# A new written-out order of the loop's tasks in an eight-element transformer layer

## The reference

```python
x = x + attn(layernorm(x))             # 16 heads of 16, two masked score entries, softmax over 512
x = x + xattn(layernorm(x), ctx_1024)  # own layernorm inside, 16 heads of 64, 64 keys, tanh(gate)
x = x + ffn(layernorm(x))
# ffn: a = entmax15(layernorm(x @ proj))             16 routing weights for each token
#      h = gelu(((xb @ Win1) * (a @ C1)) @ Wout1.T)  1024 wide, rank 128
#      y = ((hb @ Win2) * (a @ C2)) @ Wout2.T
```

## Time and profile before

| | |
|---|---|
| Time, median of 3 runs | 1042.75 us (1039.65 to 1044.42) |
| Profiled execution, its own time | 1039.97 us |
| Its span, first to last instruction | 1038.2 us |
| PE, DVE, ACT busy over the span | 94%, 74%, 59% |
| One turn of the loop | 114.2 us |
| Granted TensorE clock, mean over the span | 0.990 |

### The profile page before, as it was taken

The page is one execution under the profiler, slowest core; times in us unless marked ns, Lnnn a source line. Parts: engine busy times, 40 slices in busy tenths (PEclk is TensorE's granted clock), DMA queues, the critical chain, the costliest instruction groups (busy, mean ns, idle before and its releaser), DMA issues.

```text
span 1038.2 us, 15873 instructions
## 1 busy us (share of the span) xinstructions
PE 973.4 (94%) x5238; PEld 573.0 (55%) x5238; DVE 769.5 (74%) x1610; ACT 615.5 (59%) x857; POOL 150.7 (15%) x177
## 2 busy tenths in 40 slices
PE   5779999999989999999999999999999998999898
PEld 4434434556545645565556654565556554566676
DVE  3466756897799758985798759985898769737874
ACT  2336767555566666656665676656665675664533
POOL 2000000021012200221012100220021101311320
PEclk9889999999999999999999999999999999999999
DMA  6486885824420062112611061114411160023001
GB/s 168 119 254 218 256 262 175 266 50 122 91 75 22 11 170 56 52 32 46 179 51 30 11 182 51 31 31 124 100 51 31 30 174 21 1 82 82 1 1 42
DMA packets 77930, 97.38 MB, mean 94 GB/s; under 512 B 10383, under 2 KB 60370, under 8 KB 76850
## 3 DMA queue, kind: packets, MB, share of 16 engines
q1 hardware_dynamic: 77874, 96.69, 33.1%
HBM read 41.41 MB, written 29.36 MB: 68 GB/s over the span
## 4 chain that ended last, share of the span: by engine, by line
PE 62%; DVE 18%; ACT 7%; issue 6%; SPq 4%; DMA 2%; POOL 0%; ACTq 0%; DVEq 0%; POOLq 0%
PE y_ps L984 22%; PE x_ps L984 16%; PE pv_ps L984 7%; PE st_ps L984 7%; PE sm_ps L984 5%; DVE mx L1625 4%; PE y_ps L1147 3%; SPq L832 2%; ACT probs L1421 2%; PE y_ps L1113 2%; DVE stat L1645 1%; DVE qk_lo L1680 1%; DVE res L1697 1%; DMA a_scr<-a_cat 1%; ACT L1421 1%
## 5 line engine op out<-in xcount | busy, mean ns | idle before, releaser
L1625 DVE TENSOR_REDUCE mx<-sm_ps 128x2 f32<-128x1024 f32 x256 | 312.2, 1219 | 113.9 <-PE sm_ps L984 113.4
L1421 ACT ACTIVATE probs<-st_ps 128x1024 f32<-128x1024 f32 x256 | 262.4, 1025 | 178.0 <-PE st_ps L984 172.0
L984 PE MATMUL pv_ps<-probs,v_all 128*32 128x512 f32 x1024 | 135.9, 607 | 0.4 <-ACT o_t L1421 0.4
L984 PE MATMUL st_ps<-q_st,k_st 52*128 52x512 f32 x512 | 124.2, 480 | 2.1 <-ACT probs L1421 1.8
L984 PE MATMUL sm_ps<-k_st,q_st 50*128 50x512 f32 x512 | 118.5, 454 | 7.6 <-DVE mx L1625 5.3
L984 PE MATMUL x_ps<-b_cat,pt 128*128 128x256 f32 x448 | 112.0, 388 | 0.0
L984 PEld LDWEIGHTS st_ps<-q_st,k_st 52*128 52x128 f32 x512 | 48.4, 184 | 95.7 <-issue 55.0
L984 PEld LDWEIGHTS x_ps<-b_cat,pt 128*128 128x128 f32 x448 | 80.1, 190 | 23.9 <-issue 13.7
L699 POOL TENSOR_TENSOR px<-px,cst 128x512 f32<-128x512 f32 x56 | 58.1, 1044 | 202.2 <-DVE cst L1720 202.2
L984 PEld LDWEIGHTS sm_ps<-k_st,q_st 50*128 50x128 f32 x512 | 49.0, 186 | 69.5 <-DVE mx L1625 32.3
L1421 ACT ACT_TABLE_LOAD x60 | 77.0, 1283 | 1.8 <-PEq L2135 0.7
(11 more groups left out here) (304 smaller groups left out, 1708.3 us busy)
## 6 DMA issues: line engine op xcount, KB each, us to landing
a_scr<-a_cat SPq DMA_DIRECT2D x16, 1024.0 KB, 5.7
a_cat<-a_scr SPq DMA_DIRECT2D x8, 2048.0 KB, 8.6
q_st<-qk_hi SPq DMA_DIRECT2D x128, 64.0 KB, 2.3
k_st<-qk_hi SPq DMA_DIRECT2D x128, 64.0 KB, 2.2
b_scr<-b_cat SPq DMA_DIRECT2D x8, 1024.0 KB, 5.0
b_cat<-b_scr SPq DMA_DIRECT2D x16, 512.0 KB, 10.7
xa<-in_x SPq DMA_DIRECT2D x9, 512.0 KB, 3.9
q_st<-qk_lo SPq DMA_DIRECT2D x64, 64.0 KB, 2.2
```

The lines of the kernel that those rows point to most:

```text
L984: return nc.tensor.matmul(dst, lhs, rhs, start=start, stop=stop, **kw)
L1421: return nc.scalar.activation(dst, src, f, **kw)
L1625: nc.vector.tensor_reduce(mx[:, c % 2, 0:16].rearrange("p (m x) -> p m x", m=2)[:, :, col], sm_ps[:], axis=AX, op=ALU.max).then_inc(sm_tak ...
```

## The change

It puts the 179 entries of LOOP_PE, 83 of LOOP_ACT, 113 of LOOP_DVE and 13 of LOOP_SP in other orders; no entry is added or taken away. Two edits outside the lists: ScalarE, before it writes xt_hi in ON 0, waits for PJ 0 and Z1 1 of the element before (their matmuls read xt_hi); and the gated result of the very last step lies in px instead of in probs. EARLY_*, LAST_* and TAIL_* stay. In the new orders:

- TensorE: the OT, Y and ON steps move forward, QK0 moves from after M2 to after M7 and QK3 from before OT 2 to just ahead of M13. H0 moves from right behind P24 to behind QK 2 part 0. ZM5 to ZM7 now end the turn. 27 P and M pairs stand side by side instead of 26, and 10 P or M stand alone instead of 12.
- ScalarE: the Exp and Gelu users alternate less: 6 changes of table in a turn instead of 10.
- VectorE: EN1 and Z2 come ahead of M0, EN0 comes after M29.
- Queue: ST comes first; FS0 and FS1 after MR0; RS and FS2 now behind MR2; LA and LB now behind FS3, and MR3 behind these.

```diff
 LOOP_PE = (
-    ("P", 0, 0), ("M", 0, 0), ("V", 0, 0), ("V", 0, 1), ("V", 1, 0), ("V", 1, 1), ("X1", 0, 0), ("TN", 0, 0),
-    ("PV", 15, 0), ("P", 2, 0), ("M", 1, 0), ("X1", 1, 0), ("OT", 0, 0), ("P", 4, 0), ("M", 2, 0), ("QK", 0, 0),
...
-    ("M", 11, 0), ("G", 0, 0), ("P", 22, 0), ("G", 1, 0), ("PV", 4, 0), ("M", 12, 0), ("P", 24, 0), ("H", 0, 0),
-    ("P", 26, 0), ("M", 13, 0), ("PV", 5, 0), ("X2", 0, 0), ("X2", 1, 0), ("M", 14, 0), ("H", 1, 0), ("M", 15, 0),
...
+    ("M", 0, 0), ("P", 0, 0), ("V", 0, 0), ("V", 0, 1), ("TN", 0, 0), ("V", 1, 0), ("V", 1, 1), ("M", 1, 0),
+    ("X1", 0, 0), ("PV", 15, 0), ("M", 2, 0), ("P", 2, 0), ("OT", 0, 0), ("OT", 1, 0), ("X1", 1, 0), ("M", 3, 0),
+    ("P", 4, 0), ("OT", 2, 0), ("OT", 3, 0), ("P", 6, 0), ("M", 4, 0), ("PV", 0, 0), ("P", 8, 0), ("Y", 0, 0),
+    ("Y", 1, 0), ("P", 10, 0), ("PV", 1, 0), ("M", 5, 0), ("P", 12, 0), ("ON", 0, 0), ("ON", 1, 0), ("P", 14, 0),
+    ("M", 6, 0), ("PV", 2, 0), ("PV", 3, 0), ("P", 16, 0), ("M", 7, 0), ("QK", 0, 0), ("QK", 0, 1), ("P", 18, 0),
...
+    ("QK", 2, 0), ("H", 0, 0), ("H", 1, 0), ("QK", 2, 1), ("H", 2, 0), ("M", 12, 0), ("S", 0, 0), ("S", 0, 1),
+    ("S", 1, 0), ("S", 1, 1), ("P", 30, 0), ("S", 2, 0), ("S", 2, 1), ("S", 3, 0), ("S", 3, 1), ("QK", 3, 0),
+    ("QK", 3, 1), ("M", 13, 0), ("P", 32, 0), ("T", 0, 0), ("S", 4, 0), ("S", 4, 1), ("T", 1, 0), ("O", 0, 0),
+    ("M", 14, 0), ("P", 34, 0), ("PV", 7, 0), ("M", 15, 0), ("P", 36, 0), ("O", 0, 1), ("O", 0, 2), ("S", 5, 0),
+    ("S", 5, 1), ("O", 0, 3), ("P", 38, 0), ("M", 16, 0), ("T", 2, 0), ("S", 6, 0), ("S", 6, 1), ("TN", 2, 0),
...
+    ("PV", 13, 0), ("PV", 14, 0), ("M", 30, 0), ("P", 60, 0), ("Z1", 0, 0), ("Z1", 1, 0), ("P", 62, 0), ("M", 31, 0),
+    ("ZM", 5, 0), ("ZM", 6, 0), ("ZM", 7, 0))
...
 LOOP_DVE = (
...
+    ("EN", 1), ("Z2", 0), ("M", 0), ("TN", 0), ("EN", 2), ("EN", 3), ("M", 1), ("X1", 0), ("M", 2), ("OT", 0),
...
+    ("X2", 1), ("M", 11), ("QK", 2), ("M", 12), ("C", 0), ("C", 1), ("SU", 0), ("C", 2), ("C", 3), ("SU", 1),
+    ("QK", 3), ("SU", 2), ("M", 13), ("M", 14), ("C", 4), ("M", 15), ("C", 5), ("M", 16), ("SU", 3), ("SU", 4),
...
 LOOP_SP = (
-    ("XA", 0), ("FS", 0), ("MR", 0), ("ST", 0), ("FS", 1), ("MR", 1), ("FS", 2), ("MR", 2), ("LA", 0), ("LB", 0),
-    ("RS", 0), ("FS", 3), ("MR", 3))
+    ("ST", 0), ("XA", 0), ("MR", 0), ("FS", 0), ("FS", 1), ("MR", 1), ("MR", 2), ("RS", 0), ("FS", 2), ("FS", 3),
+    ("LA", 0), ("LB", 0), ("MR", 3))
...
         def z2_gated(g):
 
-            return probs[:, 0, 0, :] if g.reg is None and g.off == B else z1g
+            return px[:, 1].rearrange("p h s -> p (h s)")[:, 0:N] if g.reg is None and g.off == B else z1g
...
+                    if kind == "ON" and i == 0 and not is_first(g):
+                        filled(act, g + -1, "PJ", 0)
+                        filled(act, g + -1, "Z1", 1)
                     y, read = filled(act, g, kind, i), done(g, kind, i)
```

## The result

The changed kernel takes 1013.24 us (median of 4 runs, 1011.12 to 1015.33), the kernel before 1043.49 in the same comparison. The ratio is 0.9717, with a 95% interval from 0.9679 to 0.9755: 2.8% faster. The forecast was 1032 with a range from 1018 to 1045. So the direction was right, and the gain is almost three times what I worked out: 28.8 us of span instead of 10.

What follows compares the result with a forecast made beforehand. TensorE, with work for 109.97 of 114.00 us, bounds the kernel. Per turn 3.1 added - 4.9 waiting - 0.5 standing alone = -2.3, taken as -2.0; five turns give -10 us, so 1032 us, range 1018 to 1045.

Steps and rivals of the forecast that it cites:

- What bounds the kernel, the direction: TensorE sets the turn; its eight waits of the old order, costing 4.9 us a turn, all go.
- H0, H1: TensorE's two large waits, 1.09 and 0.67 us, vanish in the new order; X2 counted 0, up to 0.5 us.
- Sum of what is added: 3.1 us: New TensorE waits a turn: TN0 0.7, P after P 0.8, M20 and OT0 0.4, M16 1.2 us.
- M16: TensorE waits 1.2 us for FS0's rows: 11.6 us after QK3 against 10.4 us of its own work.
- Standing alone. Together 0.5: On TensorE, two fewer lone P or M save 0.2 us, three joined parts of O and PJ 0.3.
- I hold back 0.3: Reserve of 0.3 us a turn for late starts the walk does not see, turning -2.3 into -2.0.
- Table loads, nothing: Four fewer table loads a turn take 5.1 us off ScalarE, but nothing more is counted for the turn.
- The queue: The moved transfers arrive in time: RS and FS2 need 13.5 of about 19 us; LA and LB have 45 us.
- Rival 1: MR3's maximum rows, queued behind LA and LB, reach P16 too late; 1050 us at a 28 us landing; chance 0.15.
- Rival 2: Each wait that goes is replaced (M16 2 us, TN0 1.5, VectorE behind): 1042 +- 4; chance 0.20.
- Rival 3: FS0 in time and VectorE ahead, nearly all waiting goes: -4 to -5 us a turn, 1018 to 1022; chance 0.14.
- Theory A: From the follow-ups: TensorE's waits went because all engines' and the queue's orders fit each other; ScalarE's total work is of no account.

Runs made afterwards that it cites:

- e2: The kernel before with H0 moved behind the second X2 on TensorE and ScalarE: 1057.6 us, ratio 1.0114.
- e5: The changed kernel with QK3 one step later, on TensorE behind P32 and on VectorE behind M13: 1025.54 us.
- e14: The changed kernel with four more borders between TensorE steps that are not P, M or PV (T5, ZM4, TN3 moved): 1018.82 us.
- e15: The kernel before with nine moves on TensorE alone that join steps of a kind, ten borders fewer: 1050.20 us, ratio 1.0059.
- e9: The changed kernel with four joined TensorE groups taken apart (P2, P16, P52, M20 moved), eight more borders: 1025.88 us.
- e1: The kernel before with GT0 moved on ScalarE to just ahead of H0, 8 table loads a turn instead of 10: 1043.66 us, ratio 0.9993.
- e3: The changed kernel with GT1 moved on ScalarE to behind P46, 8 table loads a turn instead of 6: 1013.59 us.
- e4: The changed kernel with GT0 moved on ScalarE to behind P10, 8 table loads a turn instead of 6: 1034.04 us.
- e7: The kernel before with the changed kernel's order of transfers, only XA still ahead of ST: 1041.92 us, ratio 0.9987.
- e8: The changed kernel with LA and LB earlier in the queue, M4 and M6 ahead of P, T2 ahead of M16, TN0 behind the following V: 1016.59 us.
- e12: The changed kernel with M0 ahead of Z2 on VectorE, M6 ahead of P14 on TensorE, LA and LB earlier in the queue: 1011.50 us.
- e13: The changed kernel with M0 ahead of Z2 on VectorE and LA and LB earlier in the queue: 1010.31 us.
- e10: The changed kernel with M4 ahead of P6 and M6 ahead of P14 on TensorE: 1015.97 us.
- e6: The changed kernel with FS0 ahead of MR0 in the transfer queue: 1089.62 us.
- e11: The changed kernel with M0 ahead of Z2 on VectorE, nothing else: 1009.53 us, ratio 0.9686.

## Why the prediction was off, by its own steps

**What bounds the kernel, the direction:** right. TensorE sets the turn, the eight waits of the old order are gone from their places, and the turn followed. What waiting costs (4.9 us) stands for turn 3. Turns 4 and 5 of the kernel before have six such waits, so there it is 3.6 + 0.7 = 4.2 us.

**H0, H1:** right, no wait is left, and X2 has none either. e2 adds that this could not be had by moving H0 behind X2.

**The step that failed, first: "Sum of what is added: 3.1 us".** It is about 1.2 in the trace: TN0 0.3 for 0.7, P after P 0.2 + 0.3 for 0.8, OT0 0.1 for 0.1, M20 nothing for 0.3, M16 0.26 for 1.2. For TN0, 5.6 us passed from M31 at 383.39 to TN0 at 389.01, where I had 5.9 (and my terms for TensorE add up to 5.1, not 5.2). For P after P the rows of ScalarE's timeline show the two errors:

```profile
401.43 1.02 ACT L1421 ACTIVATE probs<-st_ps 128x1024 f32<-128x1024 f32 x1 [1.25 <-PE st_ps L984]
402.35 0.59 ACT L1421 ACTIVATE x1t_hi<-x_ps 128x512 fp32r<-128x512 f32 x1
403.17 1.02 ACT L1421 ACTIVATE probs<-st_ps 128x1024 f32<-128x1024 f32 x1 [0.22 <-PE st_ps L984]
404.79 1.02 ACT L1421 ACTIVATE probs<-st_ps 128x1024 f32<-128x1024 f32 x1 [0.60 <-PE st_ps L984]
```

The exp starts 403.17 - 402.65 = 0.52 us after its P, not 0.61, and the next P starts 404.24 - 403.17 = 1.07 after it, not 1.03 + 0.13. For M16 the queue's side was shorter and TensorE's longer than in my sum. TensorE has finished QK3 at 434.49 us, where M13 starts. The rows of the queue, FS0's first issue and its last:

```profile
436.32 1.28 SPq L832 DMA_DIRECT2D q_st<-qk_hi  x2
...
443.35 0.59 SPq L832 DMA_DIRECT2D k_st<-qk_hi  x1
```

VectorE took 436.32 - 434.49 = 1.8 us (I had 1.7), the issues 7.0 (7.4), and M16 started 2.35 after the last: 11.2 us for my 11.6. TensorE's own steps between took 445.44 - 434.49 = 10.95 us for my 10.4, where 445.44 is the end of P38 at its pace; PV7 and S5, for one, took 1.16 and 1.58 us ahead of a M and of an O, for my 1.0 and 1.4. Each of these waits is a small difference of two longer sums; the one side was taken too long and, for M16, the other too short. That made a wait out of what was nearly an even race. e5 confirms that the race is that close: a step later costs 1.9 us a turn.

**The step that failed, second: "Standing alone. Together 0.5".** If 4.9 us were saved and 1.2 added, the remainder of turn 3's 5.8 us is 2.1; in turns 4 and 5 it is 5.6 - 4.2 + 1.2 = 2.6. I had counted two lone P or M and three joined parts at 0.1 us. The new order has 15 borders fewer. At the 0.05 to 0.08 us of e14 and e15 they give 0.8 to 1.2, at the 0.14 to 0.17 of e9 2.1 to 2.6, but e9's price may be that of the pairs it takes apart, and the new order has only two lone P or M fewer. So the effect was the right one and counted at too few places; that it makes up the whole remainder is not shown.

**"I hold back 0.3":** nothing of the kind appeared.

**Table loads, nothing:** right, by e1 and e3. e4 adds that the place, not the number, must be looked at.

**The queue:** right that RS, FS2, LA and LB are covered, and that it is worth nothing itself (e7).

**Rival 1, maximum rows late behind 3 MB:** it happens once, in LAST. The rows of the queue there, between FS3's first issue and P16:

```profile
818.17 1.20 SPq L832 DMA_DIRECT2D q_st<-qk_hi  x2
...
826.76 0.51 SPq L811 DMA_DIRECT2D a_cat<-a_scr  x1
827.38 1.61 SPq L820 DMA_DIRECT2D b_cat<-b_scr  x2
829.04 4.39 SPq L841 DMA_DIRECT2D q_st<-nm  x4
```

P16 gets its rows 840.53 - 818.17 = 22.4 us after FS3's first issue; my sum had 22.5 after P62, which is 22.0 after that issue. LAST asks for them 0.97 us before that, turn 3 asks 406.86 - 383.59 = 23.3 us after its FS3 and doesn't wait. If the rows land as late there, which the trace doesn't show, the loop's margin is about 0.9 us, half of what I had, and enough. The rule of the Trainium skill that the prediction cited (page "DMA: Bandwidth & Descriptors", section "Queues, rings and completion order"), that a transfer's semaphore write lands only after the earlier writes of its DMA engine, fits this: with LA ahead of MR2 and LB ahead of RS the wait is gone (e8, e12, e13).

**Rival 2, a wash:** it didn't come. M16 was 0.26 us late for its 2, TN0 0.3 for its 1.5, and no M behind the block of C and SU waits.

**Rival 3, nearly all waiting goes:** this is what came. I gave it 0.14, because "the P distances above are plain arithmetic". They were, with a distance that was 0.2 us too long. Even so, its 4 to 5 us a turn left out the fall of the busy time, and the measured time lies below its 1018.

What stays open: why the cost of a step changes with its neighbours, and how much of the 2.6 to 2.8 us of busy time the borders carry. Theory A is supported by what failed (H0, nine steps of TensorE, the table loads or the queue, each moved alone, brought nothing or cost time), but no run gives a single engine its whole new order, so which of the lists the gain needs is not shown either.

## What to carry to other kernels

Where one engine is 96% busy, its busy time is not fixed. Count how often the order changes between kinds of steps and price the change from rows where the same step stands before different neighbours, as carefully as the waits. A forecast wait that is the difference of two sums of 6 to 12 us is uncertain by its own size; take its lower bound as seriously as its upper. Be wary of mending a local wait in a hand-made order by moving the step that waits: that made the turn longer here each time (e2, e8, e10), while making the work earlier that it waits for (M0 ahead of Z2), tried at one place, gained what it promised and more.

## What was not expected of the hardware

- A single wait of 2.78 us of TensorE was followed, about 1 us after it had gone on, by a little over 3 us at a granted clock of 0.50, 1.2 instead of 2.4 GHz, which added 1.4 us to the turn. Shorter waits can do it too. In turn 3 of e1 it came behind a wait of 1.70 us, in e5 (at 786 us) behind one of 1.77, and in e15 behind two of 1.46 and 1.39. In turn 5 of e15:

```profile
665.25 0.49 PE L984 MATMUL y_ps<-z_hi,wout_hi 128*128 128x512 f32 x1 [1.46 <-DVE z_lo L1615]
...
667.00:668.00 1.00, 1.00 (x8) 0.00 (x0) 1.00 (x3) 0.00 (x0) 0.38 (x1) 0.50 0.00 0
```

- Yet the wait of 1.39 us in turn 4 of e15 (at 550 us) left the clock at 1.00, and so did the waits of up to 1.3 us in turns 4 and 5 of the other runs. So no length of wait divides the two cases here. In e6, behind a wait of 13.2 us, the clock of the turn was 0.93 to 0.94.
- The same matmuls were busy for 107.5 us (e11) to 110.9 us (e2) in a turn at the full clock, by the order of the lists alone.
- An instruction's row of ScalarE or VectorE runs about 0.1 us into that of the next. The exp of the changed kernel at 401.43 us (1.02 long, shown above) is followed by the next instruction at 402.35, 0.92 us later, and VectorE's QK3 at 435.45 (0.70 long) by the next at 436.07, so durations of rows must not simply be added up.
